# Routing weights of a mixture-of-experts front stage as repeated rows brought by transfers instead of by a matmul

## The chip, the cores and the metric

The kernel runs on one core of a Trainium2 chip. Its engines each have a queue of their own and work through it in order: TensorE (PE, matmuls; PEld is its weight load), VectorE (DVE), ScalarE (ACT), GpSimd (POOL) and SyncE (SP, which here only issues DMA transfers). An engine waits on semaphores that others count up. SBUF is the on-chip memory of 128 partitions, PSUM the banks that TensorE writes. The metric is the device time in microseconds (us), median of several runs.

## The reference, cut to what matters

The input is x of 16 batches, 512 tokens and 128 features. Six sublayers follow one another. The front of the kernel computes the first four, the back the last two (a softmax attention and an MLP), which the change does not touch.

```
x = x + 0.5 * moe(layernorm(x))          # 16 experts of width 64, top 2, and a shared one of 128
x = x + linear_attention(layernorm(x))   # silu(q), silu(k) turned by angles, (q k^T) v, norm, gate u
x = x + 0.5 * moe(layernorm(x))          # same weights
x = x + 0.5 * mlp(layernorm(x))          # relu, width 512
x = x + attention(layernorm(x))
x = x + 0.5 * mlp(layernorm(x))
# moe:
scores = sigmoid(x @ gate.T); w, idx = top_k(scores, 2); w = w / (w.sum() + 1e-20)
comb[token, idx] = w                      # 16 weights a token, all but two of them zero
y = sum_e comb[:, e] * ((silu(x @ Wg[e]) * (x @ Wu[e])) @ Wd[e]) + shared(x)
```

## The kernel before

**Tiles and banks.** Everything of the front lies transposed: features or expert columns on the 128 partitions, the 512 tokens of a batch along the free axis. A pair of experts (2 x 64 columns) fills the partitions, so one MoE layer on one batch is 9 tiles n = 0 to 8: tile 0 the shared expert, tiles 1 to 8 a pair each. In each tile TensorE makes the gate product into `G[n % 2]` (three 128x512 matmuls, high and low parts, line 712 to 714), then the up product into `U`, which has one bank. ScalarE makes `s = silu(G)` (line 410). VectorE multiplies `su = U * s` (line 566, `activated`) and then `h = C * su` (line 575, `routed`), where C is the routing weight of each token, repeated over the 64 partitions of its expert. TensorE makes C with one 128x512 matmul a tile (line 747, `routing_weights`) from `cT`, the transposed weights, and `w_pairs`, a 0/1 matrix. One tile later TensorE adds `h @ Wd` to `Y` (line 719, `moe_down`, four matmuls that the profile records as eight).

**Slots.** The front is 34 slots. A slot is one MoE layer on one batch (the main work) beside one side job on the other batch: linear attention or MLP in turn. 16 slots have attention at their side, 16 the MLP, and the first and the last have none. Which side job is done where is written out by hand, tile by tile, in one function `slot` for each engine.

**Preparing the next slot.** In each slot the main input of the next is prepared: statistics (VectorE, `main_stats`), normalisation on GpSimd (`main_normalise`, into z), transposes of z into the bank `Z` and its high and low part (`main_high` on ScalarE, `main_low` on VectorE), router logits, the exponential for the sigmoid (`scores`, line 379), and on VectorE four steps of the top-2 choice (`routing_scores`, `routing_best`, `routing_next`, `routing_weights`). The table `PREPARE` says at which tile each step stands, for an attention slot and an MLP slot. The exponential and silu lie in different tables of ScalarE, so `scores` brings two table loads. The weights `comb` are transposed by TensorE at tile 0 of the slot that uses them (line 737), and ScalarE copies them to `cT` (line 413).

**The side job.** Its input is normalised by ScalarE (`zs`, line 383) with scale and offset from GpSimd (`side_start`), transposed at tile 2 (line 755), and split into `xhs` and `xls` (line 588). In an attention slot the keys, values and gate follow at tiles 3 and 4 (line 779 to 781), the query product behind tile 4, key times value behind tile 5 (line 793), and at tile 6 the product of queries with the masked result `kvm` (line 802, `attend`; the mask is line 623 on VectorE, which stands ahead of `activated` of tile 6).

Of the kernel before, what the change touches and what calls it, by code (L numbers as in the profile page):

```python
# [56 lines left out]
class Chain:  # L57
# [39 lines left out]
    MLP: {"statistics": 2, "transpose": 4, "low": 4, "logits": 5, "scores": 6, "best": 6, "next": 7, "weights": 8},  # L97
    ATT: {"statistics": 1, "transpose": 3, "low": 3, "logits": 4, "scores": 5, "best": 6, "next": 7, "weights": 8},
# [8 lines left out]
def build_front(nc, weights, x_dram, mid_dram, ident_dram, turns):  # L107
    w = weights
    with ExitStack() as ctx:
# [45 lines left out]
        comb = sb("comb", [P, T, E])  # L155
        comb2 = sb("comb2", [P, T, P])
        combh = sb("combh", [P, T, E], F32R)
        cT = [sb(f"cT{p}", [P, T, P], F32R) for p in range(2)]

        sbuf_s = [sb(f"s{p}", [P, T, P]) for p in range(2)]  # L160
# [22 lines left out]
        U = ps("U", [P, T, P])  # L183
        C = ps("C", [P, T, P])
# [25 lines left out]
        weight_ready = sig("weight_ready", TE * NM, TE)  # L210
# [34 lines left out]
        oT_ready = sig("oT_ready", N_ATT)  # L245
        comb_cleared = ctx.enter_context(nc.semaphore("comb_cleared"))
# [5 lines left out]
        block = ctx.enter_context(nc.Block())  # L252

# [6 lines left out]
        def _(sp):  # L260
# [17 lines left out]

            load(0, -1, 2)
            if turns > 2:  # L280
                for i in range(turns - 2):
                    store(i, 1)
                    load(i, 1, i * 2 + 3)
                    store(i, 3)
                    load(i, 3, i * 2 + 4)
            store(turns - 2, 1)
            load(turns - 2, 1, 2 * turns - 1)
            store(turns - 2, 3)

            load(turns - 2, 3, 2 * turns - 2)  # L290
            store(turns - 1, 1)
            store(turns - 1, 3)
# [8 lines left out]
        def _(pool):  # L301
# [29 lines left out]
            def side_start(m, i, k):  # L331
                scale_offset(rstd_s, off_s, vpe_s, mv_s, smv_ready, smv_ready.at(i, k + 1), srstd_ready)

                pool.wait_ge(side_done.sem, side_done.at(i, k))
# [29 lines left out]
            side_start(1, turns, 0)  # L364

        @block.scalar
        def _(act):
# [36 lines left out]
            def slot(m, i, side, prepare):  # L404
                g0, steps = NT * m, PREPARE[side or MLP]
                for n in range(NT):
# [10 lines left out]
                    if n == 1 and side:  # L417
                        side_normalise(m, i, m)
# [1328 lines left out]
```

## Time and profile before

| | us |
|---|---|
| three runs | 2092.15, 2095.85, 2098.02 |
| median | 2095.85 |
| the profiled execution, its own time | 2089.9 |
| its span, first to last instruction | 2087.8 |
| span of the front, up to the last slot's end | about 1155 |

The profile is of one execution. Its page gives each engine's busy time and the costliest groups of instructions; the trace behind it can be asked for stretches, waits and a timeline. A row of the timeline begins with the start and the duration in us, and what stands in brackets at its end is how long the engine had been idle before it and who ended that. A row of stretches gives for each engine the busy us and the number of instructions, then TensorE's granted clock (1.00 is 2.4 GHz), and the DMA share and rate. In the front nearly everything repeats from slot to slot; the slots between 400.77 and 467.05 us (one attention, one MLP) are used below as the pattern.

### The profile page before, as it was taken

The page shows a single profiled execution, that of the slowest core. Times are in us where ns is not written, and L with a number is a line of the kernel's source. Part 1 is how long each engine was busy: PE and PEld are TensorE (multiplying, and loading weights), DVE is VectorE, ACT ScalarE, POOL GpSimd, SP SyncE. Part 2 cuts the span into 40 slices and gives each one's busy share as a digit, 9 for nine tenths or more (in the row PEclk, how much of TensorE's full clock was granted, in tenths as well). Part 3 has the DMA queues.
Part 4 walks back from the last instruction along what each step waited for, and adds up shares of the span by engine and source line. Part 5 has one row for each costly group of instructions (what it writes and reads, how often), then busy time and mean ns, then how long its engine had stood idle before and what let it go on. Part 6 is the DMA issues. An engine that isn't in the chain of part 4 may idle for free. (4 is left out here: it accounts for less than half of the span.)

```text
span 2087.8 us, 34428 instructions
## 1 busy us (share of the span) xinstructions
PE 1933.9 (93%) x12468; PEld 1335.6 (64%) x12468; DVE 1537.2 (74%) x3852; ACT 1174.1 (56%) x2215; POOL 670.3 (32%) x767
## 2 busy tenths in 40 slices
PE   3999999999999999999999478999999999999997
PEld 2888888888888888888888323444444444444443
DVE  5767686666767677676776168888888888888881
ACT  3444444444444444444443137888887888878874
POOL 2333343234333343333431212333333333333311
PEclk9999999999999999999999659999999999999998
DMA  3000000000000000000000122222222222222210
GB/s 125 6 11 11 1 11 11 11 1 11 11 11 11 1 11 11 11 11 1 11 6 6 36 78 90 84 85 85 86 82 79 85 85 85 79 81 85 80 47 11
DMA packets 49992, 85.81 MB, mean 41 GB/s; under 512 B 6752, under 2 KB 11104, under 8 KB 49760
## 3 DMA queue, kind: packets, MB, share of 16 engines
q1 hardware_dynamic: 47920, 81.85, 12.5%
q8 instruction: 99, 1.62, 0.3%
q10 hardware_dynamic: 1904, 1.78, 0.3%
q14 instruction: 69, 0.57, 0.1%
HBM read 49.26 MB, written 34.87 MB: 40 GB/s over the span
## 5 line engine op out<-in xcount | busy, mean ns | idle before, releaser
L1344 DVE TENSOR_REDUCE b_nm<-b_MX 128x1 f32<-128x512 f32 x1024 | 649.6, 683 | 101.8 <-PE b_MX L1459 93.7
L1235 ACT ACTIVATE b_pr<-b_ST 128x512 f32<-128x512 f32 x1024 | 550.1, 601 | 153.6 <-PE b_ST L1446 151.1
L410 ACT ACTIVATE s<-G 128x512 f32<-128x512 f32 x306 | 182.7, 597 | 350.9 <-PE G L714 348.2
L1459 PE MATMUL b_MX<-b_kt,b_qt 32*128 32x512 f32 x1024 | 350.4, 505 | 22.1 <-DMA b_qt<-staging 11.6
L719 PE MATMUL Y<-w_wd,h 128*128 128x128 f32 x2448 | 329.0, 277 | 17.4 <-DVE h L575 16.1
L1446 PEld LDWEIGHTS b_ST<-b_qt,b_kt 32*128 32x128 f32 x1024 | 126.7, 183 | 320.4 <-ACT b_pr L1235 209.8
L1446 PE MATMUL b_ST<-b_qt,b_kt 32*128 32x512 f32 x1024 | 313.1, 497 | 19.8 <-ACT b_pr L1235 18.7
L566 DVE TENSOR_TENSOR su<-U,s 128x512 f32<-128x512 f32 x272 | 187.0, 687 | 190.6 <-PE U L714 113.5
L719 PEld LDWEIGHTS Y<-w_wd,h 128*128 128x128 f32 x2448 | 305.8, 192 | 33.2 <-DVE h L575 23.9
L1474 PE MATMUL b_PV<-b_pr,b_va 128*32 128x512 f32 x2048 | 276.2, 612 | 0.0
L575 DVE TENSOR_TENSOR h<-C,su 128x512 f32<-128x512 f32 x272 | 188.0, 691 | 9.3
L1459 PEld LDWEIGHTS b_MX<-b_kt,b_qt 32*128 32x128 f32 x1024 | 139.8, 186 | 56.0 <-DVE b_nm L1344 30.8
L314 POOL TENSOR_TENSOR vpe_s<-mv_s,w_eps 128x4 f32<-128x4 f32 x33 | 6.6, 201 | 451.4 <-DVE mv_s L470 451.4
L712 PE MATMUL G<-xh,w_wgh 128*128 128x512 f32 x306 | 145.6, 476 | 0.0
L712 PE MATMUL U<-xh,w_wuh 128*128 128x512 f32 x306 | 123.7, 404 | 9.5 <-DVE su L566 9.5
L714 PE MATMUL G<-xl,w_wgh 128*128 128x512 f32 x306 | 121.1, 396 | 0.0
L713 PE MATMUL G<-xh,w_wgl 128*128 128x512 f32 x306 | 120.9, 395 | 0.0
L714 PE MATMUL U<-xl,w_wuh 128*128 128x512 f32 x306 | 120.7, 394 | 0.0
L713 PE MATMUL U<-xh,w_wul 128*128 128x512 f32 x306 | 120.3, 393 | 0.0
L747 PE MATMUL C<-cT,w_pairs 128*128 128x512 f32 x272 | 107.6, 396 | 0.0
L401 ACT ACTIVATE hs<-S,w_b 128x512 f32<-128x512 f32 x68 | 46.8, 688 | 104.2 <-PE S L714 104.2
L1132 POOL TENSOR_TENSOR b_ve<-b_mv,w_eps_two 128x4 f32<-128x4 f32 x16 | 3.2, 203 | 301.8 <-DVE b_mv L1270 301.8
(246 smaller groups left out, 3492.4 us busy)
## 6 DMA issues: line engine op xcount, KB each, us to landing
b_kt<-staging SPq DMA_DIRECT2D x64, 256.0 KB, 2.8
b_qt<-staging SPq DMA_DIRECT2D x64, 256.0 KB, 3.4
staging<-b_khi SPq DMA_DIRECT2D x32, 256.0 KB, 3.0
staging<-b_qhi SPq DMA_DIRECT2D x32, 256.0 KB, 3.2
xin<-in_x SPq DMA_DIRECT2D x17, 256.0 KB, 2.9
mid<-xo SPq DMA_DIRECT2D x17, 256.0 KB, 2.0
b_x<-mid SPq DMA_DIRECT2D x16, 256.0 KB, 3.1
staging<-b_klo SPq DMA_DIRECT2D x16, 256.0 KB, 3.1
```

The source lines that it names most:

```text
L410: nc.scalar.activation(sbuf_s[n % 2][:], G[n % 2][:], ACT.Silu).then_inc(act_done.sem, 1)
L566: nc.vector.tensor_tensor(out[:], U[:], sbuf_s[n % 2][:], ALU.mult).then_inc(up_used.sem, 1)
L575: nc.vector.tensor_tensor(h[n % 3][:], C[:], su[n % 2][:], ALU.mult).then_inc(h_ready.sem, 1)
L712: pe.matmul(flat(bank), wh, flat(high), start=True, stop=False)
L713: pe.matmul(flat(bank), wl, flat(high), start=False, stop=False)
L714: return pe.matmul(flat(bank), wh, flat(low), start=False, stop=True)
L719: mm = pe.matmul(bank[:, t], hid[:, t], wd, start=(first and t == 0), stop=True, skip_group_check=True)
L1235: nc.scalar.activation(pr[k % 2][:, j], bank[:].rearrange("p a b -> p (a b)"), ACT.Exp, scale=SM_SCALE).then_inc(used["st"].sem, 1)
L1344: nc.vector.tensor_reduce(nm[g % 2][:, c:c + 1], bank[:].rearrange("p a b -> p (a b)"), AX.X, ALU.max).then_inc(used["mx"].sem, 1)
L1446: pe.matmul(flat(ST[place % ST_BANKS]), kt_[g][rows_of(j), k % T], flat(qt[g])[rows_of(j)], start=True, stop=True).then_inc(made["st"].sem, 1)
L1459: pe.matmul(flat(MX[place % MX_BANKS]), qt[g][rows_of(j), u // HG % T], flat(kt_[g])[rows_of(j)], start=True, stop=True).then_inc(made["mx ...
L1474: mm = pe.matmul(flat(PV)[rows_of(j)], va[B.parity][:, kt, g * HG + j], pr[k % 2][:, j], start=(kt == 0), stop=(kt == T - 1), skip_group_c ...
```

## The change

The weight matmul and its bank C are gone. TensorE transposes `comb` at tile 8 of the slot before; ScalarE copies its 16 rows to `cT`; SP writes them to a DRAM buffer `spread` (one transfer) and reads them back with 16 transfers, each one expert's row repeated over 64 partitions, into `cw[p]`, of which there are two. `routed` multiplies by a slice of `cw`, so both its inputs lie in SBUF. The freed bank is the second one of `U`; `s` has three buffers in place of two. The high and low split of `comb` is gone (three small VectorE instructions a slot). In `PREPARE` most steps stand a tile or more sooner. The first statistics of an attention slot's successor are made at the end of the MLP slot ahead of it. `main_high` and `main_low` now come ahead of the side job's two parts of the same tile. The side transposes stand behind `moe_down` of tile 2 in place of ahead of it. GpSimd does the next main normalisation ahead of `side_start` in attention slots, and the bias addition behind both.

```diff
 PREPARE = {
-    MLP: {"statistics": 2, "transpose": 4, "low": 4, "logits": 5, "scores": 6, "best": 6, "next": 7, "weights": 8},
-    ATT: {"statistics": 1, "transpose": 3, "low": 3, "logits": 4, "scores": 5, "best": 6, "next": 7, "weights": 8},
+    MLP: {"statistics": 1, "transpose": 3, "low": 3, "logits": 4, "scores": 6, "best": 6, "next": 7, "weights": 7},
+    ATT: {"statistics": None, "transpose": 2, "low": 2, "logits": 3, "scores": 5, "best": 6, "next": 7, "weights": 7},
 }
...
-        U = ps("U", [P, T, P])
-        C = ps("C", [P, T, P])
+        U = [ps(f"U{k}", [P, T, P]) for k in range(2)]
...
+            def spread_weights(q, i):          # SyncE
+                k = number(q, i)
+                p = k % 2
+                sp.wait_ge(cT_ready.sem, cT_ready.at(i, q + 1))
+                if k >= 2:
+                    for n in range(TE):
+                        sp.wait_ge(spread[n], 32 * (k - 1))
+                sp.dma_start(spread_dram[p], cT[p][:].rearrange("e t p -> e (t p)")).then_inc(rows_out, 16)
+                if k >= 2:
+                    sp.wait_ge(h_ready.sem, TE * (k - 1))
+                sp.wait_ge(rows_out, 16 * (k + 1))
+                for n in range(TE):
+                    for e in range(2):
+                        sp.dma_start(cw[p][e * I_E:(e + 1) * I_E, n].rearrange("p t q -> p (t q)"),
+                                     spread_dram[p][2 * n + e:2 * n + e + 1].broadcast_to([I_E, N])
+                                     ).then_inc(spread[n], 16)
...
                 for m in range(NM):             # GpSimd
-                    side_start(m, i, m)
-                    main_normalise(m + 1, i)
+                    if SIDE[m] == ATT:
+                        main_normalise(m + 1, i)
+                        side_start(i, m)
+                    else:
+                        side_start(i, m)
+                        main_normalise(m + 1, i)
+                    side_bias(m, i, m)
...
+            def weight_rows(q, i):             # ScalarE, behind s of tile 8
+                k = number(q, i)
+                act.wait_ge(combT_ready.sem, combT_ready.at(i, q + 1))
+                if k >= 2:
+                    act.wait_ge(rows_out, 16 * (k - 1))
+                nc.scalar.activation(cT[k % 2][:], Z[0:E], ACT.Copy).then_inc(cT_ready.sem, 1)
...
             def routed(m, n, i):               # VectorE
...
-                dve.wait_ge(weight_ready.sem, weight_ready.at(i, c0 + n))
+                dve.wait_ge(spread[n - 1], 32 * (k + 1))
                 if n >= 3:
                     dve.wait_ge(down_done.sem, down_done.at(i, g0 + n - 2))
-                nc.vector.tensor_tensor(h[n % 3][:], C[:], su[n % 2][:], ALU.mult).then_inc(h_ready.sem, 1)
+                nc.vector.tensor_tensor(h[n % 3][:], su[n % 2][:], cw[k % 2][:, n - 1], ALU.mult).then_inc(h_ready.sem, 1)
...
+                    if prepare and n == steps["low"]:      # now ahead of side_low, in the tile loop
+                        main_low(m + 1, i)
                     if n == 2 and side:
                         side_low(i, m)
...
+                if prepare and side != ATT and not (m == NM - 1 and i == turns - 1):
+                    main_stats((m + 2) % NM, i + (m + 2) // NM)
+                if side:
+                    dve.wait_ge(xb_ready.sem, xb_ready.at(i, m + 1))
                 main_residual(m, i)
...
-                    if n >= 1:                  # TensorE
-                        pe.wait_ge(up_used.sem, up_used.at(i, g0 + n))
-                    product(U, w["wuh"][:, n], w["wul"][:, n], high, low).then_inc(up_ready.sem, 1)
-                    if n == 0:
-                        comb_transposes(m, i)
-                        if side == MLP:
-                            out_transposes(nth(m - 1), i)
-                    else:
-                        routing_weights(m, n, i)
+                    if n >= 2:
+                        pe.wait_ge(up_used.sem, up_used.at(i, g0 + n - 1))
+                    product(U[n % 2], w["wuh"][:, n], w["wul"][:, n], high, low).then_inc(up_ready.sem, 1)
+                    if prepare and n == steps["weights"] + 1:
+                        comb_transposes(m + 1, i)
...
             main_transposes(-1, 0)
             logits(-1, 0)
+            comb_transposes(-1, 0)
             slot(-1, 0, None, True)
```

**What moved, on ScalarE.** In an attention slot before, from s of tile 4 on (`kvu` is the silu of the keys, `qa` of the queries, `lb` and `en` belong to the next slot's router; a table load carries the line of the instruction it is for):

```order
L410 ACTIVATE s<-G 128x512 [waits up_used,gate_ready]
L425 ACTIVATE kvu<-kvu 128x4x128 [waits kvu_out]
L427 ACTIVATE qa<-S,w_bq 128x512 [waits q_mm]
L375 ACTIVATE lb<-Z 128x64 [waits logits_ready]
L410 ACTIVATE s<-G 128x512 [waits up_used,gate_ready]
L379 ACT_TABLE_LOAD
L379 ACTIVATE en<-lg 128x64 [waits lg_ready]
L410 ACT_TABLE_LOAD [waits up_used]
L410 ACTIVATE s<-G 128x512 [waits gate_ready]
L410 ACTIVATE s<-G 128x512 [waits up_used,gate_ready]
```

and now:

```order
L406 ACTIVATE lb<-Z 128x64 [waits logits_ready]
L448 ACTIVATE s<-G 128x512 [waits up_used,gate_ready]
L462 ACTIVATE kvu<-kvu 128x4x128 [waits kvu_out]
L464 ACTIVATE qa<-S,w_bq 128x512 [waits q_mm]
L410 ACT_TABLE_LOAD
L410 ACTIVATE en<-lg 128x64 [waits lg_ready]
L448 ACT_TABLE_LOAD [waits up_used]
L448 ACTIVATE s<-G 128x512 [waits gate_ready]
```

The table loads and `en` stood behind s of tile 5; they now stand ahead of it, right behind `qa`. `lb` stood behind `qa` and now stands ahead of s of tile 4.

**On VectorE.** Tiles 2 and 3 of an attention slot before (`xls` is the side input's low part, `xl` the next main input's):

```order
L566 TENSOR_TENSOR su<-U,s 128x512 [waits up_ready,act_done]
L575 TENSOR_TENSOR h<-C,su 128x512 [waits weight_ready,up_used]
L588 TENSOR_TENSOR xls<-S,xhs 128x512 [waits xhs_ready]
L566 TENSOR_TENSOR su<-U,s 128x512 [waits h_ready,up_ready,act_done]
L575 TENSOR_TENSOR h<-C,su 128x512 [waits down_done,weight_ready,up_used]
L612 TENSOR_TENSOR kvu<-S,w_bkvu 128x384 [waits kvu_mm] x2
L491 TENSOR_TENSOR xl<-Z,xh 128x512 [waits xh_ready]
```

and now:

```order
L595 TENSOR_TENSOR su<-U,s 128x512 [waits up_ready,act_done,h_ready]
L605 TENSOR_TENSOR h<-su,cw 128x512 [waits spread1,up_used]
L529 TENSOR_TENSOR xl<-Z,xh 128x512 [waits xh_ready]
L618 TENSOR_TENSOR xls<-S,xhs 128x512 [waits xhs_ready]
L595 TENSOR_TENSOR su<-U,s 128x512 [waits up_ready,act_done,h_ready]
L605 TENSOR_TENSOR h<-su,cw 128x512 [waits down_done,spread2,up_used]
L642 TENSOR_TENSOR kvu<-S,w_bkvu 128x384 [waits kvu_mm] x2
```

`xl` stood behind the tile's products and the `kvu` additions of tile 3 and now stands ahead of `xls`.

**On TensorE.** The end of an attention slot and the start of the MLP slot before, from the last weight matmul on:

```order
L747 MATMUL C<-cT,w_pairs 128x512 [waits h_ready]
L719 MATMUL Y<-w_wd,h 128x128 [waits h_ready]
L719 MATMUL Y<-w_wd,h 128x128 x3
L719 MATMUL Y<-w_wd,h 128x128 [waits h_ready]
L719 MATMUL Y<-w_wd,h 128x128 x3
L712 MATMUL G<-xh,w_wgh 128x512 [waits xl_ready]
L713 MATMUL G<-xh,w_wgl 128x512
L714 MATMUL G<-xl,w_wgh 128x512
L712 MATMUL U<-xh,w_wuh 128x512
L713 MATMUL U<-xh,w_wul 128x512
L714 MATMUL U<-xl,w_wuh 128x512
L737 MATMUL Z<-w_ident,comb 128x128 [waits comb_ready]
```

and now, from the up product of tile 8 on:

```order
L747 MATMUL U<-xh,w_wuh 128x512 [waits up_used]
L748 MATMUL U<-xh,w_wul 128x512
L749 MATMUL U<-xl,w_wuh 128x512
L772 MATMUL Z<-w_ident,comb 128x128 [waits comb_ready]
L772 MATMUL Z<-w_ident,comb 128x128 x3
L754 MATMUL Y<-w_wd,h 128x128 [waits h_ready]
L754 MATMUL Y<-w_wd,h 128x128 x3
L754 MATMUL Y<-w_wd,h 128x128 [waits h_ready]
L754 MATMUL Y<-w_wd,h 128x128 x3
L747 MATMUL G<-xh,w_wgh 128x512 [waits xl_ready]
```

The transposes of `comb` stood behind the next slot's first two products and now stand ahead of this slot's last two groups into `Y`. The weight matmul is gone from each of tiles 1 to 8.

## Rows read from the trace of the kernel before

**Rows 1.** The page, busy time of each engine: us (share of the span) instructions

```profile
PE 1933.9 (93%) x12468; PEld 1335.6 (64%) x12468; DVE 1537.2 (74%) x3852; ACT 1174.1 (56%) x2215; POOL 670.3 (32%) x767
```

**Rows 2.** Stretches: us, busy (count) of PE PEld DVE ACT POOL, clock, DMA share, GB/s

```profile
400.77:433.43 32.66, 31.41 (x204) 27.88 (x203) 25.69 (x75) 14.26 (x26) 17.17 (x20) 1.00 0.05 18
433.43:467.05 33.62, 32.98 (x214) 28.75 (x212) 21.25 (x66) 14.89 (x25) 6.30 (x9) 1.00 0.01 1
```

**Rows 3.** Waits between 110 and 1150 us: who for whom, total, times, longest

```profile
PE Y L719 <- DVE h L575: 13.8, 15, 0.9
...
PE U L712 <- DVE su L566: 9.0, 16, 0.6
```

**Rows 4.** Timeline of PE, an attention slot's tile 7: start, duration, engine, line, operation

```profile
427.80 0.39 PE L747 MATMUL C<-cT,w_pairs 128*128 128x512 f32 x1
428.03 1.05 PE L719 MATMUL Y<-w_wd,h 128*128 128x128 f32 x8
428.84 0.49 PE L712 MATMUL G<-xh,w_wgh 128*128 128x512 f32 x1
```

**Rows 5.** Timeline of all engines, attention slot, query product to attend

```profile
417.04 0.48 PE L712 MATMUL S<-xhs,w_wqh 128*128 128x512 f32 x1
...
418.02 0.69 ACT L427 ACTIVATE qa<-S,w_bq 128x512 f32<-128x512 f32 x1 [0.69 <-PE S L714]
...
419.33 1.28 ACT L379 ACT_TABLE_LOAD   x1
...
419.46 0.69 DVE L566 TENSOR_TENSOR su<-U,s 128x512 f32<-128x512 f32 x1 [0.38 <-PE U L714]
420.19 0.69 DVE L575 TENSOR_TENSOR h<-C,su 128x512 f32<-128x512 f32 x1
...
420.90 1.28 ACT L410 ACT_TABLE_LOAD   x1
420.91 0.80 DVE L503 TENSOR_SCALAR en<-en 128x64 f32<-128x64 f32 x1
...
422.91 0.41 DVE L623 TENSOR_TENSOR kvm<-S,w_heads 128x256 f32<-128x256 f32 x1
...
423.73 0.49 PE L802 MATMUL S<-kvm,qc 128*128 128x128 f32 x3
```

**Rows 6.** Timeline of DVE behind attend, same slot

```profile
428.09 0.68 DVE L566 TENSOR_TENSOR su<-U,s 128x512 f32<-128x512 f32 x1
...
430.31 0.22 DVE L540 TENSOR_TENSOR share<-sc,den 128x64 f32<-128x64 f32 x1
```

**Rows 7.** Timeline: the side input's low part and its first reader

```profile
409.03 0.68 DVE L588 TENSOR_TENSOR xls<-S,xhs 128x512 fp32r<-128x512 f32 x1
...
410.31 0.33 PE L779 MATMUL S<-w_wkvuh,xhs 128*128 128x384 f32 x1
```

**Rows 8.** Three lines over the whole run: min/median/max ns, first and last start

```profile
L544 DVE TENSOR_TENSOR first<-first,second x34: 212/217/929, 40.2 to 1129.3; 128x64 f32<-128x64 f32 x34
...
L348 POOL TENSOR_TENSOR kc<-kvu,w_sin_t x16: 1797/1798/1801, 85.8 to 1080.6; 128x512 f32<-128x512 f32 x16
...
L352 POOL TENSOR_TENSOR qc<-qa,w_cos_c x16: 1267/1271/1275, 87.6 to 1082.4; 128x512 f32<-128x512 f32 x16
```

**Rows 9.** Timeline of POOL and DVE in the MLP slot

```profile
446.64 1.04 POOL L329 TENSOR_TENSOR z<-z,rstd 128x512 f32<-128x512 f32 x1
...
459.81 0.19 DVE L503 TENSOR_SCALAR en<-en 128x64 f32<-128x64 f32 x1 [2.64 <-ACT en L379]
...
462.31 0.68 DVE L566 TENSOR_TENSOR su<-U,s 128x512 f32<-128x512 f32 x1
```

**Rows 10.** An issue on the SP queue, and issues by form from the page

```profile
404.51 0.43 SPq L277 DMA_DIRECT2D xin<-in_x  x1
...
xin<-in_x SPq DMA_DIRECT2D x17, 256.0 KB, 2.9
mid<-xo SPq DMA_DIRECT2D x17, 256.0 KB, 2.0
```

More of the change, by code:

```diff
@@ L154, in build_front @@
         den = sb("den", [P, T, 1])
[L155 to L160, printed above, removed]
+        comb = sb("comb", [P, T, P])
+        cT = [sb(f"cT{p}", [E, T, P]) for p in range(2)]
+        cw = [sb(f"cw{p}", [P, TE, T, P]) for p in range(2)]
+        sbuf_s = [sb(f"s{p}", [P, T, P]) for p in range(3)]
         su = [sb(f"su{k}", [P, T, P]) for k in range(2)]
@@ L245, in build_front @@
         oT_ready = sig("oT_ready", N_ATT)
+        spread = [ctx.enter_context(nc.semaphore(f"spread{n}")) for n in range(TE)]
+        rows_out = ctx.enter_context(nc.semaphore("rows_out"))
         comb_cleared = ctx.enter_context(nc.semaphore("comb_cleared"))
@@ L252, in build_front, with number, wait_for @@
         block = ctx.enter_context(nc.Block())
+        slots = NM * turns + 2
+        def number(m, i):
+            return NM * i + m + 1
+        def wait_for(eng, signal, i, n):
+            if signal.at(i, n) > 0:
+                eng.wait_ge(signal.sem, signal.at(i, n))
         def source(q):
@@ L277, in load @@
                 sp.dma_start(xin[p][:], xd[batch]).then_inc(x_loaded[p].sem, 16)
-            load(0, -1, 2)
[L280 to L292, printed above, removed]
+            def spread_weights(q, i):
[14 more added lines that the diff above has]
+                                     ).then_inc(spread[n], 16)
+            spread_weights(-1, 0)
+            spread_weights(0, 0)
+            load(0, -1, 2)
+            for i in range(turns):
+                for m in range(NM):
+                    spread_weights(m + 1, i)
+                    if m % 2 == 1:
+                        store(i, m)
+                        if i < turns - 1:
+                            load(i, m, min(i * 2 + 3 + m // 2, 2 * turns - 1 - m // 2))
             sp.wait_ge(side_done.sem, side_done.at(turns, 1))
@@ L418, in slot @@
                         side_normalise(m, i, m)
+                    if prepare and n == steps["transpose"]:
+                        main_high(m + 1, i)
                     if n == 2 and side:
@@ L439, in slot @@
                             scores(m + 1, i)
+                        if n == steps["weights"] + 1:
+                            weight_rows(m + 1, i)
             main_high(-1, 0)
@@ L443, in _ @@
             scores(-1, 0)
+            weight_rows(-1, 0)
             slot(-1, 0, None, True)
@@ L658, in slot @@
                             main_stats(m + 1, i)
-                        if n == steps["low"]:
-                            main_low(m + 1, i)
                         if n == steps["logits"]:
@@ L831, in slot @@
                         down(S[1], oT, w["wout"][:], True).then_inc(side_mm.sem, 1)
-                    if n == 2 and side:
-                        side_transposes(i, m)
                     if n == 3 and side:
@@ L853, in slot @@
                         moe_down(m, n - 1, i)
+                    if n == 2 and side:
+                        side_transposes(i, m)
                     if side == ATT:
@@ L1533, in build_weights @@
     sb("router", [P, 2 * E], F32R)
-    sb("pairs", [P, TE, P], F32R)
     for name, shape in parts.items():
```

73 lines of the change are left out of this document (27 added, 46 removed).

## The prediction

> **What bounds the kernel now.** First the table of engines: PE is busy for 93% of the span, DVE for 74% [rows 1]. Then the two slots of the pattern: PE is busy for 31.41 of 32.66 us in the attention slot and 32.98 of 33.62 in the MLP slot, at clock 1.00 [rows 2]. So TensorE sets the pace of the front, and the waits say how fully: per attention slot it waits 0.9 us for h near the slot's end, per MLP slot 0.6 us for VectorE to free the one bank of U [rows 3]. A pair of slots is 66.28 us, and 16 pairs are half of the run.
>
> That average hides chains with little slack. VectorE is busy for 25.69 of 32.66 us in an attention slot [rows 2] and works in order, and in each slot there is one stretch where it runs from one instruction to the next. Taking work from TensorE helps only where such a chain does not end later. I therefore walk through each slot twice, once by TensorE's work and once by the chain, and take the later one. T is the start of a slot on PE.
>
> **The weight matmul.** C starts at 427.80 and the next matmul at 428.03, so one costs 0.23 us of PE though its row says 0.39 (matmuls overlap) [rows 4]. Eight a slot are 1.9 us, 34 slots 63 us. This is what the change can give on TensorE; the second bank of U can give the 0.6 us more. The small VectorE instructions that go lie where TensorE is not waiting, except at the slot's end.
>
> **Attention slot, start to the query product.** Before, the query product starts at 417.04, T+16.3 [rows 5]. `xls` starts at 409.03 and lasts 0.68; the product that needs it starts 0.60 later, at 410.31 [rows 7]. Now `main_low`, as long as any 128x512 product on DVE (0.69 and the gap, 0.72), stands ahead of it, while C and the `comb` transposes no longer hold TensorE there. The chain (zs, s of tile 2, su, h, xl, xls) ends at about T+9.8; TensorE arrives at T+8.4 and waits. From there the `kvu` additions behind `h` of tile 4 release the query product at T+16.3 again. Nothing gained: 0, from -0.6 (TensorE's work alone would give -0.9, less 0.3 of the chain) to +0.6 (a port wait, below).
>
> **Attention slot, query product to attend.** Here the moved table loads tell. Before, qa 418.02, s of tile 5, then the loads, while VectorE made su and h of tile 5 from 419.46 on, and the router's scores from 420.91; the mask started at 422.91 and attend at 423.73, 6.69 us behind the query product [rows 5], with TensorE not waiting. Now s of tile 5 stands behind both loads. The chain from the start of the query product: 0.98 to qa (418.02 - 417.04), 0.71 qa, then 2.87 for load, exponential, load (419.33 to 420.90 + 1.28 and a gap), 0.62 s, 1.45 su and h (419.46 to 420.91), 2.00 scores (420.91 to 422.91), 0.41 mask, 0.1 to PE: 9.1 us [rows 5]. TensorE itself would be there after 6.2 (6.69 less two C). So +2.4 against 6.69. The second bank of U cannot help: attend stands in order on PE, and the mask in order on DVE. At least +1.8: the first score instruction took 0.80 for the 0.19 of its twin in the MLP slot [rows 5, 9], and only that 0.6 could go.
>
> **The shared port.** `routed` now reads two SBUF operands; before, one was the PSUM bank C. Three lines bear on that: `first + second` (L544), both inputs in SBUF, has a median of 217 ns and takes up to 929 while GpSimd works; GpSimd's product for the keys, which starts 0.04 behind VectorE's for the keys, takes 1798 ns in all 16, and its like 1271 [rows 8]. So one can hold the other for the rest of its instruction, at most 1.27 us of GpSimd. GpSimd is busy for 17.17 of 32.66 us in an attention slot and 6.30 of 33.62 in an MLP slot [rows 2]. With a mean rest of 0.6 us (half of 1.27), eight `routed` wait 8 x 0.53 x 0.6 = 2.5 us in an attention slot and 0.9 in an MLP slot if each meets GpSimd by chance and all lies on the chain; the least is 0. GpSimd is busy without a gap while h of tile 5 is made, so I add 0.4 there, near the low end since most other meetings lie where VectorE has slack.
>
> The Trainium skill (SBUF — State Buffer, "Who interferes with whom") says that a VectorE instruction with two SBUF inputs contends with a GpSimd instruction that reads SBUF, and whoever comes second blocks until the other ends. By that rule every meeting counts in full, and that is the fourth rival below; the trace agrees with 929 against 217 ns [rows 8].
>
> The Trainium skill (ScalarE: Activation LUTs, "What ACT_TABLE_LOAD costs") puts a switch of tables at about 2.66 us with its drain; two would be 5.3. An estimate by it makes the attention slot 2.5 us longer still. The trace has 1.28 and the next instruction at once [rows 5], so the sum does without it.
>
> **Attend to the end of the attention slot.** Before, 9.7 us (423.73 to 433.43, with 0.9 of waiting). Now VectorE is behind: attend to su of tile 7 takes 4.36 (428.09), from there to the end of `share` 2.44 (430.31 + 0.22) [rows 5, 6], then `first` and `comb` 0.47 free or 1.2 held by GpSimd as now, transposes of `comb` 0.5, two groups into Y 0.81 + 0.91: 9.5 to 10.2 against 9.7. C's two are saved but the transposes have to wait for the weights. I take +0.2. Sum of the attention slot: 0 + 2.4 + 0.4 + 0.2 = +3.0.
>
> **MLP slot.** TensorE alone would end 1.9 to 2.5 us sooner. Two chains stand against that. `main_stats` comes about 3.6 us sooner, so z, done at 447.68 or T+14.2 [rows 9], is done at about T+10.7, where TensorE, one tile ahead of before, arrives at T+10.1: 0.7 lost. From there TensorE needs 8.4 to the third hidden product (the tile's 0.23 and 0.81 steps of rows 4). Then relu 0.75, load, exponential and load 2.87, s of tile 6 0.62, su and h 1.45 [rows 5], scores and best 2.50 (459.81 to 462.31) [rows 9], su and h 1.4, next and weights 1.5, `comb` transposes 0.5, and three groups 2.5 behind them: T+10.8 + 8.4 + 0.75 + 2.87 + 0.62 + 1.45 + 2.5 + 1.4 + 1.5 + 0.5 + 2.5 = 33.3. Against 33.62: -0.3, from -1.9 (no chain) to +0.9 (each `routed` held). The VectorE wait of 2.64 for the exponential [rows 9] goes, since `scores` stands a tile sooner there on ScalarE, but the weights are wanted 4 us sooner too. `main_stats` at the slot's end takes the place of the weight instructions there.
>
> **Transfers.** Per slot one of 32 KB out, then 16 of 128 KB. A 256 KB transfer lands in 2.9 us, one to DRAM in 2.0, and issuing takes 0.43 on SP [rows 10], where nothing else of the front waits but two transfers in two slots with a slot of time. `cT` is ready 1.2 to 1.7 ahead of the slot's end, the rows are out at T+1, the first pair lands at T+4.5, and `routed` of tile 1 wants it at T+4.2. Later pairs come every 0.9 us and are wanted every 3. Cost 0 to 0.3, hidden by su of tile 1; if a repeated row comes slower than an ordinary one it costs (rival three).
>
> **Ends.** The first slot starts behind the `comb` transposes, about +2.5; it and the last save 1.9 each on PE: -1.
>
> **Sum.** 16 x (3.0 - 0.3) - 1 = +42 on the profiled 2089.9: 2132. The median is 6 us above that execution; I put the forecast between, at 2134.
>
> **Rivals.** *TensorE stays the bound.* If the chains have the slack that 93% suggests, C and the waits go: 34 x 1.9 = 64 to 34 x 2.7 = 92 us less, 2000 to 2030. It decides if attend starts within 6.3 us of the query product. For it: busy shares and the small waits [rows 1 to 3]; against: the sum of 9.1 is of rows alone. 0.12. *Balance.* The attention slot loses its least, 1.8, and the MLP slot gains its most, 1.9: 2090. Against it is that z and the exponential would have to be free there. 0.08. *Late rows.* The 16 reads of one DRAM row each, or the way out and back, take 2.5 us longer; `routed` of tile 1 and all behind it on VectorE (side residual, `main_stats`, z) go later by 2.4 in the MLP slot and 0.5 in the attention slot: +46, 2180. For it: no transfer of before repeats a row or waits for another to DRAM and back; against: a DMA share of at most 0.05 now [rows 2]. 0.08. *Port in full.* 16 x (2.5 + 0.9) = +54 in place of the 6 taken: 2180. 0.12. The forecast has the remaining 0.60.
>
> **Range and chances.** The forecast's own bounds are 16 x (1.8 - 0.6 - 1.0) = +3 (the attention terms at their least, the MLP slot half way to no chain) and 16 x (3.7 + 0.6 + 0.5) = +77 (h of tile 5 held by 1.27, the first stretch by 0.6, the MLP slot half way to its end), so 2093 to 2167. To hold 8 in 10 the range takes in part of the two late cases and leaves the fast one out: 2093 to 2180. Within 0.3%, 6 us, a measurement of this kernel cannot tell a change. Faster: 0.12 + 0.02 of the balance + 0.02 = 0.16. Same: 0.05. Slower: 0.79.
>
> **What would show it.** In the timeline after: ScalarE's s of tile 5 some 4 us behind the query product's end, VectorE idle for it, and TensorE waiting 2 to 3 us at attend for the mask. At tile 8 it waits for `comb`, one to two us. `routed` has instructions longer than 0.69 us, or GpSimd's are longer. The pair of slots is near 69 us in place of 66.28. It is wrong if TensorE meets attend without waiting, if the tile 8 transposes don't wait, or if `routed` of tile 1 waits for its rows by more than a us.

## The result, and the profile after

| | before | after |
|---|---|---|
| median us (lowest to highest) | 2094.32 (2092.15 to 2098.02), 4 runs | 2228.11 (2226.19 to 2229.83), 4 runs |
| profiled execution, its span | 2089.9, 2087.8 | 2229.83, 2228.0 |
| mean granted clock of TensorE | 0.977 | 0.952 |

The ratio is 1.0637 [1.0617, 1.0656]: 134 us slower. The sign was forecast, the size was not: +38 us on the median shown was predicted, and 2228 lies outside the range that ended at 2180.

The engines' table, to set against [rows 1], then the group of the new `routed` with its issues of transfers:

```profile
PE 1936.2 (87%) x12196; PEld 1334.5 (60%) x12196; DVE 1557.1 (70%) x3749; ACT 1173.5 (53%) x2215; POOL 696.0 (31%) x767
...
L605 DVE TENSOR_TENSOR h<-su,cw 128x512 f32<-128x512 f32 x272 | 206.0, 758 | 10.5 <-DMA cw<-spread 1.1
...
cw<-spread SPq DMA_DIRECT2D x544, 128.0 KB, 3.0
```

272 matmuls are gone and TensorE is busy for as long as before, 1936.2 us against 1933.9. So some of the remaining ones run slower: the page's mean for one of `moe_down` is 292 ns, and 277 before. The rows of weights come in time: `routed` waited for them 1.1 us in the whole run.

I cut both spans at the residual addition that ends each slot's main work on VectorE (line 609 after, 579 before). Of the 140.2 us between the spans, 125.1 lie in the 16 attention slots (mean 40.86 against 33.04 us), 3.9 in the 16 MLP slots (33.53 against 33.29), 7.9 in setup and first slot, -2.1 in the last, and 5.4 in the back. So it is one kind of slot. Columns as in [rows 2], three neighbouring slots of after (attention, MLP, attention), and one of before on the same marks:

```profile
376.32:414.01 37.69, 30.62 (x195) 26.55 (x194) 25.87 (x66) 14.16 (x26) 16.99 (x19) 1.00 0.22 71
414.01:447.42 33.41, 31.16 (x204) 27.18 (x203) 22.00 (x69) 14.89 (x25) 8.01 (x11) 1.00 0.22 65
447.42:489.81 42.39, 34.69 (x195) 30.74 (x194) 26.36 (x65) 14.26 (x26) 16.99 (x19) 0.88 0.19 63
```

```profile
401.05:434.09 33.04, 31.79 (x204) 28.18 (x203) 26.27 (x78) 14.26 (x26) 17.17 (x20) 1.00 0.05 17
```

The two attention slots hold the same instructions. One takes 37.69 us at clock 1.00, the other 42.39 at 0.88. Three of the 16 are of the first kind (37.7 to 37.8 us); the other 13 take 40.8 to 42.4 at 0.88 to 0.92. All slots of before are at 1.00. Where in the slot the clock is lost, same columns:

```profile
447.42:473.60 26.18, 21.22 (x129) 18.21 (x127) 16.88 (x36) 10.98 (x19) 12.78 (x13) 0.98 0.30 100
473.60:479.00 5.40, 5.37 (x25) 5.40 (x26) 2.68 (x13) 0.00 (x0) 0.19 (x1) 0.50 0.01 3
479.00:485.60 6.60, 3.92 (x21) 3.00 (x20) 5.53 (x17) 2.70 (x6) 4.02 (x6) 0.98 0.00 0
485.60:489.80 4.20, 4.17 (x22) 4.12 (x23) 1.27 (x2) 0.59 (x1) 0.00 (x0) 0.59 0.04 10
```

Twice the clock is at the lower of its two levels, 1.2 GHz (0.50), and each time TensorE has just waited. PE's timeline shows the waits in brackets and what follows; the same two places of the slot at full clock stand below it:

```profile
473.63 3.75 PE L827 MATMUL S<-kvm,qc 128*128 128x128 f32 x16 [3.45 <-DVE kvm L653]
477.18 1.91 PE L754 MATMUL Y<-w_wd,h 128*128 128x128 f32 x8
...
485.63 0.69 PE L772 MATMUL Z<-w_ident,comb 128*128 128x128 f32 x4 [2.72 <-DVE comb L585]
486.12 3.58 PE L754 MATMUL Y<-w_wd,h 128*128 128x128 f32 x16
```

```profile
402.53 2.02 PE L827 MATMUL S<-kvm,qc 128*128 128x128 f32 x16 [3.46 <-DVE kvm L653]
404.39 1.06 PE L754 MATMUL Y<-w_wd,h 128*128 128x128 f32 x8
...
410.92 0.66 PE L772 MATMUL Z<-w_ident,comb 128*128 128x128 f32 x4 [1.80 <-DVE comb L585]
411.41 1.06 PE L754 MATMUL Y<-w_wd,h 128*128 128x128 f32 x8
```

Attend's 16 matmuls take 3.75 us behind one wait of 3.45 and 2.02 behind another of 3.46. The wait for `comb` is 1.80 us in each of the three slots at full clock and 2.6 to 2.9 in each of the other 13, so its greater length goes with the slow stretch ahead of it. The longest totals of TensorE's waits between 110 and 1280 us; before, the two longest totals were 13.8 and 9.0 [rows 3]:

```profile
PE Z L772 <- DVE comb L585: 67.2, 32, 2.9
...
PE S L827 <- DVE kvm L653: 51.9, 15, 3.5
...
PE S L804 <- DVE xls L618: 16.3, 15, 1.1
```

The chain that makes TensorE wait at attend, from the query product on, to set against [rows 5]:

```profile
463.68 0.50 PE L747 MATMUL S<-xhs,w_wqh 128*128 128x512 f32 x1
...
464.68 0.69 ACT L464 ACTIVATE qa<-S,w_bq 128x512 f32<-128x512 f32 x1
...
465.39 1.28 ACT L410 ACT_TABLE_LOAD   x1
...
466.96 1.28 ACT L448 ACT_TABLE_LOAD   x1
...
468.25 0.60 ACT L448 ACTIVATE s<-G 128x512 f32<-128x512 f32 x1
...
468.94 0.69 DVE L595 TENSOR_TENSOR su<-U,s 128x512 f32<-128x512 f32 x1 [3.46 <-ACT s L448]
...
469.66 1.22 DVE L605 TENSOR_TENSOR h<-su,cw 128x512 f32<-128x512 f32 x1
...
470.29 1.71 POOL L387 TENSOR_TENSOR ub<-kvu,w_lnb 128x512 f32<-128x512 f32 x1
470.80 1.25 DVE L541 TENSOR_SCALAR en<-en 128x64 f32<-128x64 f32 x1
472.08 0.55 DVE L543 RECIPROCAL sc<-en 128x64 f32<-128x64 f32 x1
...
473.07 0.42 DVE L653 TENSOR_TENSOR kvm<-S,w_heads 128x256 f32<-128x256 f32 x1
```

VectorE stands idle for 3.46 us until s of tile 5 comes from behind both table loads; then `routed` takes 1.22 us and the first score instruction 1.25, while GpSimd is at work. Attend starts 9.95 us behind the query product: 6.69 before, 9.1 in the prediction.

### The profile page after: what moved, and what is told of

Read it like the earlier page. It is cut to its first block and busy times, and to the rows that moved or that the text cites. A ratio compares the mean times of both kernels' runs of the same rounds, so it can differ in the third digit from the quotient of the medians.

```text
span 2228.0 us, 34714 instructions
## 1 busy us (share of the span) xinstructions
PE 1936.2 (87%) x12196; PEld 1334.5 (60%) x12196; DVE 1557.1 (70%) x3749; ACT 1173.5 (53%) x2215; POOL 696.0 (31%) x767
## 5 line engine op out<-in xcount | busy, mean ns | idle before, releaser
L754 PE MATMUL Y<-w_wd,h 128*128 128x128 f32 x2448 | 350.1, 292 | 1.9 <-DVE h L605 1.9
L754 PEld LDWEIGHTS Y<-w_wd,h 128*128 128x128 f32 x2448 | 333.2, 207 | 12.3 <-DVE h L605 3.1
L605 DVE TENSOR_TENSOR h<-su,cw 128x512 f32<-128x512 f32 x272 | 206.0, 758 | 10.5 <-DMA cw<-spread 1.1
L331 POOL TENSOR_TENSOR vpe<-mv,w_eps 128x4 f32<-128x4 f32 x34 | 6.8, 201 | 384.8 <-DVE mv L508 384.8
L827 PE MATMUL S<-kvm,qc 128*128 128x128 f32 x256 | 47.4, 361 | 55.3 <-DVE kvm L653 55.3
L422 ACT ACTIVATE zs<-xw,off_s,rstd_s 128x128 f32<-128x128 f32 x132 | 54.4, 482 | 70.3 <-POOL off_s L344 70.3
```

Of the source, the lines that this page charges most:

```text
L605: nc.vector.tensor_tensor(h[n % 3][:], su[n % 2][:], cw[k % 2][:, n - 1], ALU.mult).then_inc(h_ready.sem, 1)
L754: mm = pe.matmul(bank[:, t], hid[:, t], wd, start=(first and t == 0), stop=True, skip_group_check=True)
```

## The experiments

Each time is compared with the kernel before, run on the same chip. A slot's time is the mean of all 16 of its kind in the profiled execution.

**One: silu of tile 5 ahead of the loads.** From after:

```diff
-                        if n == steps["logits"] + 1:
+                        if n == steps["logits"] + (2 if side == ATT else 1):
```

> The changed kernel, with one line undone: in attention slots ScalarE makes s of tile 5 ahead of the exponential and its two table loads again. Theory A (the table loads ahead of s of tile 5 hold VectorE, VectorE's mask holds attend on TensorE for 3.5 us, and behind that idle time the granted clock is at its lower level for a while): the wait at attend falls from 3.5 to at most 1 us, every attention slot shows a clock of 1.00, and the time is 16 x (3.0 + 3.2) = about 100 us less than 2228, so near 2130 (2105 to 2150). Theory B (the two SBUF operands of the routed product, or the 16 repeated-row transfers a slot, are what costs): within 20 us of 2228.

2141.75 us, ratio 1.0229 [1.0214, 1.0245]: 86 of the 134 us are gone. The attention slot is 35.47, at clock 1.00 in all but one:

```profile
354.44:389.80 35.36, 30.59 (x195) 26.55 (x194) 26.35 (x65) 14.15 (x26) 16.95 (x19) 1.00 0.23 76
```

The wait at attend is 1.17 us in place of 3.45. At full clock the slot falls from 37.7 to 35.4, so the order on ScalarE is 2.3 us of it. The other 3.1 of the mean came back with the clock.

**Two: the same order in the kernel before.**

```diff
-                        if n == steps["logits"] + 1:
+                        if n == steps["logits"] + (0 if side == ATT else 1):
```

> The kernel before, with only this changed: in attention slots the exponential and its two table loads stand ahead of s of tile 5, behind the router's copy. Theory A: attend waits 2 to 3 us, the clock falls in some attention slots, and the time rises from 2094 by 16 x 2.5 = 40 without a fall of the clock to 16 x 5.5 = 90 with it: 2134 to 2185. Theory B: no change from 2094 beyond 10 us, since nothing of the transfers and operands is in it.

2131.8, ratio 1.0186 [1.0165, 1.0206], just under the range expected. The attention slot is 2.24 us longer (35.28), the MLP slot as long as before (33.29), and the wait at attend appears:

```profile
PE S L802 <- DVE kvm L623: 22.4, 15, 1.5
```

So one moved step on ScalarE costs 39 us with all the rest left alone, 36 of them in the attention slots: the term of 2.4 of the prediction stands. Behind waits of at most 1.5 us the clock was 1.00 in 15 of the 16 attention slots and 0.95 in one.

**Three: TensorE kept at work through both waits.** From after; the products go into banks that nobody reads then:

```diff
+                        if side == ATT:
+                            pe.wait_ge(lg_ready.sem, lg_ready.at(i, m + 2))
+                            for _ in range(7):
+                                pe.matmul(flat(Z), w["wqh"][:], flat(high), start=True, stop=True)
...
+                            pe.wait_ge(qa_ready.sem, qa_ready.at(i, a + 1))
+                            for _ in range(14):
+                                pe.matmul(flat(S[1]), w["wqh"][:], flat(xhs), start=True, stop=True)
```

> The changed kernel with more work: in attention slots TensorE makes 14 products of 128x512 into a free bank ahead of attend and 7 ahead of the transposes of the weights, whose results nothing reads. They fill the two waits. Theory A with the clock as its second half: the waits of attend and of the transposes are no shorter in the end, but TensorE is not idle, the granted clock is 1.00 in all attention slots, and each is near 37.7 to 38.2 us in place of 41.2 and 42.4: 2228 - 15 x 3.3 = about 2180 (2165 to 2195), less time with 336 matmuls more. If attend's long matmuls (3.75 us in place of 2.02) come from the transfers or a port and not from the clock: 2228 or more.

2182.66, ratio 1.0428 [1.0412, 1.0443]: 336 matmuls more and 45 us less. Attention slot 38.08, 13 of them at 37.5 to 38.4, three at 39.3 and clock 0.96. One of the pattern, and attend in another:

```profile
366.62:404.35 37.73, 35.47 (x216) 30.49 (x215) 25.91 (x66) 14.15 (x26) 17.03 (x19) 1.00 0.22 71
```

```profile
463.73 2.02 PE L827 MATMUL S<-kvm,qc 128*128 128x128 f32 x16 [0.24 <-DVE kvm L653]
```

The chain is untouched (the slot is as long as that of after at 1.00); only the idle time of TensorE at attend is gone, and that for `comb` is shorter. So the clock is a cost of its own, about 3 us a slot on average. Both waits were filled together, so the run does not tell what each costs alone.

**Four and five: the port, and TensorE's own work.** Four is the kernel before with both inputs of `routed` in SBUF; five is four without the weight matmul and the waits for it. Both leave the routing weights out of the result.

```diff
-                nc.vector.tensor_tensor(h[n % 3][:], C[:], su[n % 2][:], ALU.mult).then_inc(h_ready.sem, 1)
+                nc.vector.tensor_tensor(h[n % 3][:], su[n % 2][:], su[n % 2][:], ALU.mult).then_inc(h_ready.sem, 1)
...
-                pe.matmul(flat(C), w["pairs"][:, n - 1], flat(cT[m % 2]), start=True,
-                          stop=True).then_inc(weight_ready.sem, 1)
```

> The kernel before, with the routed product reading su twice in place of the PSUM bank C and su: both operands in SBUF. It leaves out the routing weights of the result; the weight matmul is still made. Theory A: the port costs little since VectorE has slack in most places, 0 to 1 us a slot, 2094 to 2115. Theory B: 2 to 4 us a slot, 2160 to 2230.

> The kernel before with both operands of the routed product in SBUF (su twice) and without the weight matmul: 272 matmuls of 0.23 us of TensorE are gone, all else is in the order of before. It leaves out the routing weights of the result. If TensorE is the bound in the old order too: 34 x 1.9 = 64 us less than the 2116 of the kernel with the matmul, 2052, and the slots near 32.3 and 31.6. If the chains through VectorE and ScalarE are as near behind as the walk has it: under half of that, 2085 to 2105.

Four: 2116.09, ratio 1.0117 [1.01, 1.0133], attention slot 34.18 (+1.14), MLP slot 33.53 (+0.24). Five: 2106.68, ratio 1.0073 [1.005, 1.0096], attention slot 34.19, MLP slot 33.06. First the line of `routed` in four, then the same attention slot of four and of five:

```profile
L575 DVE TENSOR_TENSOR h<-su x272: 691/692/1283, 48.5 to 1176.9; 128x512 f32<-128x512 f32 x136
```

```profile
342.87:377.06 34.19, 32.53 (x205) 28.31 (x204) 27.78 (x77) 14.27 (x27) 18.60 (x20) 1.00 0.05 16
```

```profile
340.18:374.37 34.19, 30.83 (x197) 26.82 (x196) 27.98 (x77) 14.27 (x27) 18.60 (x20) 1.00 0.05 16
```

The second SBUF operand costs 22 us by the slots, 23 by the medians, where nothing else is changed: 48 of the 272 `routed` are longer than 0.72 us. GpSimd is held too: it is busy for 18.60 us in that slot and 17.17 in before's. Taking 1.7 us of matmuls out of a slot that is 95% TensorE gives nothing at all there, 0.47 in the MLP slot, and 7 to 9 us in the run, where the prediction had counted 63 us of TensorE for it. The 1.7 us came back as waits: TensorE waits in four 0.7 us for `zs` and 0.9 for the last `h` of the attention slot, in five 1.1 and 1.4, and 0.7 for the mask ahead of attend. TensorE was not the bound of the attention slot with two SBUF operands; no run takes the matmul out with C left in PSUM.

**Six to ten: can the new way be made to pay?** Each is built on the one ahead. Six is one with the `comb` transposes between the last two groups into Y instead of ahead of both. Seven puts the side job's high and low parts ahead of the main ones again. Eight puts `scores` where ScalarE would wait anyway. Nine puts `routing_scores` of the attention slot ahead of the keys' turn on VectorE. Ten does the same with `routing_best`.

```diff
-                    if prepare and n == steps["weights"] + 1:     # six, TensorE
-                        comb_transposes(m + 1, i)
...
+                if prepare:
+                    comb_transposes(m + 1, i)
                 moe_down(m, NT - 1, i)
...
+                    if prepare and side and n == steps["logits"] + 1:     # eight, ScalarE, ahead of kvu and hidden
+                        scores(m + 1, i)
...
+                            routing_scores(m + 1, i)     # nine, VectorE, in tile 4
```

> The changed kernel with s of tile 5 first and, besides, the transposes of the weights behind the second last group into Y in place of ahead of it. If the wait for the weights at tile 8 (1.8 us) is on the path: TensorE does 0.8 us of work in it, and each slot ends 0.5 to 0.8 sooner, 32 x 0.65 = 21 less than 2141, 2120 (2112 to 2128). If VectorE's h of tile 8 ends last anyway: within 8 us of 2141.

> The one before (transposes late), with the side input's high and low parts again ahead of the next main input's on ScalarE and VectorE. If TensorE's 1.1 us wait for xls in the attention slot is on the path: it falls to 0.4, 16 x 0.7 = 11 less, near 2110. If the kvu additions or the table loads behind take it up: no change beyond 5 us.

> The one before, with the exponential and its table loads where ScalarE was idle: right behind s of tile 4 in attention slots (2.6 us idle there before kvu is ready), right behind s of tile 5 and ahead of the third relu in MLP slots (1.7 us idle). If the two loads and what VectorE waits behind them are the bound of the second half of each slot: attend waits no more, s of tile 6 in the MLP slot comes 1.5 sooner, and the slots are near 33.0 and 32.0: 2060 (2040 to 2080), under both kernels. If VectorE's own work (the port included) is the bound: within 15 us of the one before.

> The kernel with the loads in ScalarE's gaps, and in attention slots VectorE's four router score instructions one tile sooner, between the kvu additions and the keys' product, where VectorE idled 1.0 us and GpSimd works on nothing. If the second half of the attention slot is VectorE's chain with its port waits (h of tile 5 took 1.76 us and the first score instruction 1.27): the first score instruction takes 0.19, attend starts 2.3 us sooner after the query product, the attention slots are near 33.6 and the time 2128 - 16 x 2.2 = 2093 (2085 to 2105). If TensorE's work or the transfers bound it: within 10 us of 2128.

> The one before, with the first five steps of the top-2 choice ahead of the statistics of attend's result, where VectorE waited 0.84 us for attend. If VectorE's chain is still the bound of the end of the slot: 0.5 to 0.8 us less an attention slot, 2083 (2072 to 2095), at or under the kernel before. If not: no change beyond 5 us.

| | us | ratio | attention slot | MLP slot |
|---|---|---|---|---|
| six | 2151.41 | 1.0277 [1.0241, 1.0313] | 36.19 | 32.80 |
| seven | 2127.31 | 1.018 [1.0157, 1.0203] | 35.58 | 32.78 |
| eight | 2128.05 | 1.0174 [1.0157, 1.0191] | 36.16 | 32.00 |
| nine | 2111.97 | 1.0087 [1.0062, 1.0111] | 35.13 | 32.08 |
| ten | 2115.24 | 1.0108 [1.0069, 1.0148] | 34.90 | 32.27 |

Six missed its gain. Its four executions took 2138.57 to 2155.33 us, and the slots of the table are of the shortest one, which is as long as the profiled one of experiment one (2138.14): the MLP slot gained 0.6 and the attention slot gave 0.7 back. Between 110 and 1280 us TensorE waits 13.5 us for `comb` in place of 55.1, but 29.1 for `h` of the last pair in place of 6.0. In an attention slot the two waits together are 2.06 us in both versions (0.90 and 1.16 against 1.79 and 0.27), since VectorE's `h` ends last; and its start became longer, with the side transposes 7.16 us into the slot in place of 6.59, behind a wait for `zs` of 0.9 in place of 0.3.

Seven had its wait for `xls` fall from 1.1 us to 0.5 and the attention slot with it by 0.6, some 10 us a run, about the 11 that were expected; the medians, with six's spread in them, fell by 24. Eight gained 0.8 in the MLP slot and lost 0.6 in the other, and the 2060 expected were missed. At attend TensorE still waits 1.2 us: GpSimd's side products hold `routed` of tile 5 for 1.76 us (1.50 in seven) and the first score instruction for 1.27 (as in seven). In some attention slots TensorE also waits 1.45 us for `h` of tile 1, whose rows come late. VectorE in eight:

```profile
367.61 0.69 DVE L597 TENSOR_TENSOR su<-U,s 128x512 f32<-128x512 f32 x1 [0.42 <-ACT s L448]
368.33 1.76 DVE L607 TENSOR_TENSOR h<-su,cw 128x512 f32<-128x512 f32 x1
370.01 1.27 DVE L543 TENSOR_SCALAR en<-en 128x64 f32<-128x64 f32 x1
```

Nine took the score instruction away from there and the wait at attend went; that gave 16 to 18 of the 35 us expected. Ten gave nothing more. In eight to ten many slots have clocks of 0.95 to 0.98, behind shorter waits than those of after.

**Eleven and twelve: matmul against rows in the same good order.** Eleven is the kernel before with its weight matmul, one bank of U and the transposes at tile 0, but with the steps, the loads and the side parts ordered as in nine (weights at tile 8). Twelve is nine with the transposes of `comb` where the change has them.

```diff
-    ATT: {"statistics": 1, "transpose": 3, "low": 3, "logits": 4, "scores": 5, "best": 6, "next": 7, "weights": 8},
+    ATT: {"statistics": None, "transpose": 2, "low": 2, "logits": 3, "scores": 5, "best": 6, "next": 7, "weights": 8},
```

> The kernel before with its weight matmul, its one bank of U and the weights' transposes at tile 0, and with what the changed order and the experiments gave: the next slot's preparation a tile or more sooner, GpSimd's order and the side transposes of the change, the table loads in ScalarE's gaps (behind s of tile 4 in attention slots, of tile 5 in MLP slots), and VectorE's router scores in the gap of tile 4. No two-operand routed product, no transfers. If both kernels are bound by the chain through the table loads and VectorE: attention slots 32.2 to 32.8 in place of 33.0 (the 0.9 us wait for h at the end goes), MLP slots 32.8 in place of 33.3 (TensorE's work with the matmul is the bound then), 2094 - 16 x 1.0 = 2078 (2065 to 2090), under both. If the order before had nothing to give: 2090 to 2105.

> The kernel with loads and scores in the gaps, with the weights' transposes back ahead of the last two groups into Y, as in the change. If the rows' late arrival (TensorE waits 1.45 us for h of tile 1 in attention slots, and VectorE waits for the transfer) is what the late transposes cost: that wait goes, attention slots lose 0.5 to 1 us, MLP slots gain 0.8 us as in the run with the transposes late, so within 8 us of 2112. If it is the clock that these waits pull down (0.97 in half of the attention slots): 2095 to 2105.

Eleven: 2094.93 (12 runs), ratio 1.0 [0.9989, 1.0012]. Twelve: 2103.02, ratio 1.0037 [1.0024, 1.005], the best of the versions with rows. A pair of slots of each, eleven first:

```profile
339.26:372.86 33.60, 32.05 (x201) 27.77 (x201) 25.03 (x70) 14.03 (x26) 17.02 (x20) 1.00 0.06 17
372.86:405.55 32.69, 32.69 (x213) 29.08 (x212) 22.09 (x73) 14.89 (x25) 6.22 (x9) 1.00 0.00 1
```

```profile
143.48:177.80 34.32, 30.55 (x195) 26.63 (x194) 26.44 (x65) 14.02 (x26) 17.14 (x19) 1.00 0.24 79
177.80:209.63 31.83, 31.16 (x204) 27.19 (x203) 22.09 (x68) 14.99 (x25) 7.81 (x11) 1.00 0.20 68
```

I had expected 2078 of eleven; its attention slot lost 0.56 and its MLP slot gained 0.66. Twelve against eleven (rows and their port, no weight matmul, the second bank of U, the earlier transposes) gives 0.65 in the MLP slot and costs 1.2 in the attention slot (34.80 on average), of which about half is clock: six of its 16 are 34.1 to 34.3 at 1.00, nine 35.0 to 35.9 at 0.93 to 0.96. In twelve no `routed` between 110 and 1280 us waits for its rows. No version beat the kernel before.

## Why the prediction was wrong in size

By its own steps, on the slots of after at clock 1.00 first, since the prediction priced nothing of the clock. Marks are the VectorE ones of the section on the result, on which the query product of before starts 15.99 us into the slot, attend 22.68 and the end is 33.04.

*Start to the query product: 0 taken, +0.27 measured* (463.68 - 447.42 = 16.26). TensorE waits 1.1 us for `xls`, as the walk had it, and the additions behind it give the time back. Right.

*Query product to attend: +2.8 taken, +3.26 measured.* Both halves were named, the silu behind the loads (2.4; experiments one and two give 2.3 and 2.24) and the port. The port is the part too small here: 0.4 taken, while `routed` of tile 5 took 0.53 more than its median and the first score instruction 1.25 where it had 0.80 before. This was the step that the walk along the chain got right and the busy shares would have hidden.

*Attend to the end: +0.2 taken, +1.12 measured* (414.01 - 402.53 = 11.48, against 10.36). The walk to the end of `share` held (6.92 against 4.36 + 2.44 = 6.80). Then `comb` took 1.25 us and `routed` of the last pair 1.19, both held beside GpSimd's products for the gate: VectorE 409.61 and 411.50 against GpSimd 409.52 and 410.87.

```profile
409.52 1.27 POOL L391 TENSOR_TENSOR og<-on,uw 128x512 f32<-128x512 f32 x1 [1.62 <-ACT on L422]
409.61 1.25 DVE L585 TENSOR_TENSOR comb<-first,share 128x64 f32<-128x64 f32 x1
...
410.87 1.27 POOL L393 TENSOR_TENSOR og<-og,ub 128x512 f32<-128x512 f32 x1
...
411.50 1.19 DVE L605 TENSOR_TENSOR h<-su,cw 128x512 f32<-128x512 f32 x1
```

The 9.5 to 10.2 of the prediction had `first` and `comb` held, but not `routed` of the last pair, and for such meetings the port's term took the low end, since "most other meetings lie where VectorE has slack". A stretch that starts behind a wait on VectorE's own chain has no slack. Experiment four gives the port by itself as 22 us in the old order, against the 6 taken and the 54 of the fourth rival. The Trainium skill (SBUF — State Buffer, "Who interferes with whom") has the rule that an operand pair in SBUF and a reading GpSimd block one another. The runs agree, with 1283 ns against 692 in experiment four; by it alone every `routed` could be held, and most were not.

Together the slot is +4.65 at full clock, 33.04 to 37.69, where +3.0 was taken: 26 us of the miss of some 95.

*The missing term.* The mean slot is 40.86, not 37.69: 3.17 x 16 = 51 us for TensorE at 1.2 GHz behind its waits. **This is the step that failed: the prediction said that TensorE would wait 2 to 3 us at attend and 1 to 2 at tile 8, saw both as idle time that was already in the chain, and never asked what the engine does when it starts again.** What follows attend on TensorE feeds VectorE (statistics of the attention product, Y, G), so the slow stretch lies on the same chain. Experiment three shows it: work without use in the waits gives 45 us back. The Trainium skill (TensorE: Matmul & The Clock Gate, "HAM oscillation — how this bites in real kernels") tells of a matmul kernel whose groups lie apart behind waits for transfers and which loses the full clock ahead of every group. The trace has the same loss behind waits for VectorE, in 13 of 16 slots, in a kernel in which TensorE is 87% busy, and the page should have been weighed against the forecast waits.

*MLP slot: -0.3 taken against 33.62, that is 33.3; 33.53 measured, +0.24.* The slot of before is 33.29 on these marks, so over 16 slots that is 9 us of the miss. But 33.62 was taken from marks on TensorE, and on those the walk held: the slot of after lasts 33.41 there.

```profile
413.66 0.48 PE L747 MATMUL G<-xh,w_wgh 128*128 128x512 f32 x1
...
447.07 0.48 PE L747 MATMUL G<-xh,w_wgh 128*128 128x512 f32 x1
```

The attention slot grows on TensorE's marks by 5.03 (32.66 to 37.69) in place of 4.65, and its stretch from attend to the end by 1.43 (9.70 to 11.13) in place of 1.12. So 6 of these 9 us belong to the attention slot, 5 of them to its end, where +0.2 was taken.

*Transfers: 0 to 0.3.* Hidden, with 1.1 us of waiting in all; the rival of late rows fell. It became real where the weights are transposed later: VectorE waits for rows about 4 us in all in six and seven, and 20 us, 16 times, in eight to ten.

*Ends: -1 taken, +5.8 measured.* The last slot is 2.1 us shorter, as forecast. The first slot cost 7.9 us more. About 2.7 of it is the tile 0 behind the `comb` transposes, as the prediction had it. Its clock (0.77 between 70 and 77.3 us) is part of the rest. Another part varies from version to version: the first slot ends between 69.4 and 79.4 us in all kernels, so it is no safe reading.

The account closes, as a sum; its last two terms are no safe readings (below for the back). The sum forecast was +42 on the profiled execution; measured were 140 between the spans: 51 clock, 26 attention slots at full clock, 9 MLP slots, 7 ends, 5 back, together 98.

The rival *TensorE stays the bound* is refuted twice: attend started 9.95 us behind the query product where 6.3 was its mark; and in the old order, with two SBUF operands, the weight matmul is worth 7 to 9 us (five against four). With C in PSUM it was not tried; there the mask ended 0.4 us ahead of attend (422.91 + 0.41 against 423.73 [rows 5]), where the two matmuls up to it are 0.46. A gain near 63 us was not there to have by this change. *Balance* fell too: the attention slot lost 4.65 us at full clock where that rival had 1.8, and the MLP slot gained nothing.

**Left open.** Three of 16 attention slots keep clock 1.00 behind the same wait of 3.46 us; no run tells what spares them. The back, which the change does not touch, takes 939.0 us against 933.6. Over the profiled executions of all kernels it takes 934 to 939, and 938.6 in eleven, which has no transfers of rows; so nothing puts the 5.4 down to the change. How much of experiment one's gain would be left at a fixed clock is known only from its slots at 1.00.

## What to carry to other kernels

Price a change by the chain that ends each stretch, not by the busiest engine: one silu moved behind two table loads cost 2.2 us a slot, more than the 1.9 that all its eight weight matmuls could give. When the walk ends in "TensorE now waits 2 to 3 us here", add a second line for what its matmuls cost at half clock behind it, and weigh moving useful work into the wait. An operand moved from PSUM to SBUF lets GpSimd hold the VectorE instruction that reads it; charge that in full wherever the chain has just been waited for.

## What the runs showed of the hardware

- TensorE fell to 1.2 GHz behind waits of 3.46 and 2.7 us inside a stream that is otherwise dense: 16 matmuls took 3.75 us for 2.02. In three slots of 16 it kept 2.4 GHz behind waits of 3.46 and 1.80. In eight to ten, slots had clocks of 0.95 to 0.98 though TensorE's waits for VectorE in the front are 2.2 us at most there.
- 336 matmuls without use, put into such waits, made the run 45 us shorter.
- A VectorE product with two SBUF operands took, beside GpSimd's products, up to 1.76 us for 0.69 (128x512, eight) and 1.25 for 0.22 (128x64, after). A 128x64 instruction with one such operand, the first of the scores, took 1.25 for 0.19.
- A transfer that repeats one row of DRAM over 64 partitions (128 KB written) lands in 3.0 us, where an ordinary one of 256 KB took 2.9 before [rows 10]; its issue on SP's queue has a median of 0.60 us against 0.43 in the row of before:

```profile
L303 SPq DMA_DIRECT2D cw<-spread x544: 444/596/1366, 47.5 to 1276.5; - x182
```
